# A gated expert layer: the first product comes out transposed, with the weight blocks stationary

## The chip, the cores and the metric

The kernel runs on one core of one Trainium2 chip. The metric is the device time of the whole program in microseconds (us), the median of a few runs. The program is written by hand for each engine: PE (matrix products), ACT (ScalarE), DVE (VectorE), POOL (GpSimd) and SP (which starts the plain DMAs). Each engine runs its own list of instructions in order; they meet only at semaphores.

## The reference

There are 2048 rows (4 batches of 512) of 512 numbers, `x`. Each row has a token number that chooses one of 4 experts. An expert is one 512 x 512 matrix `W` of `ctx_2048`, used three times:

```python
h = layernorm(x)
g = silu(h @ W.T);  u = h @ W.T          # the same product twice
y = (g * u) @ W.T
x = x + tanh(g_xattn) * y                # each row with its own expert
# second part, on every row
h2 = layernorm(x)
logits = h2 @ Wr + br + bonus            # 8 small experts, the top two, softmax weights
hid = relu(h2 @ Wd + bd)                 # 8 x 16 hidden numbers
x = x + tanh(g_ffn) * sum_e w[e] * (hid[e] @ Wu[e] + bu[e])
```

## The kernel before

**Tiling.** The kernel sorts the rows by expert and gathers them by indirect DMA in 16 tiles of 128 rows (`T`). A tile that holds rows of more than one expert is worked on once per expert, so there are `NP` = 19 pairs (tile, expert). Which expert a pair has is known only at run time: PE loads the number into a register (`expert_of`, L587) and addresses `w_hi` and `w_lo` with it.

**Precision.** Every fp32 operand of a large product is split in two fp16 halves, `hi` (ACT rounds) and `lo` (DVE subtracts), and a product is the sum of three matmuls: hi x hi, hi x lo and lo x hi. `w_hi` and `w_lo` hold the transposed weights, made once per expert at the start (`w_blocks` on PE, `high_parts` on ACT, `low_parts` on DVE and on POOL).

**One pair, engine by engine.** 
1. ACT normalises the tile into `h` (L803), PE transposes it into `ps_hT` (L656), ACT makes `hT_hi` (L789), DVE makes `hT_lo` (L1044, `hT_low`).
2. PE makes the first product in `ps_a` (`split_product`, L577 to L585): the transposed rows are stationary and 512 columns of the weights move, 12 matmuls; rows of the tile come out on the partitions.
3. ACT makes `silu` (L784), DVE the product `prod` (L1038).
4. PE transposes `prod` into `ps_pT` (`transpose_product`, L599), ACT makes `pT_hi` (L762), DVE makes `pT_lo` (L1072, `pT_low`).
5. PE makes the second product in `ps_y` with the same `split_product`; DVE adds it to the rows (L1056, `add_y`), whose tile and source numbers DVE's sequencer loads into registers (`place`, L1047).

**The second part** follows a tile when its last pair is surely done, LATE = 3 pairs later: statistics (DVE L1064, L1067, POOL L435 to L437), `h2` (ACT L775), its transposes (PE L664), `h2T_hi` and `h2T_lo` (L794, L1078), `hidden_product` (L606), the choice of two experts (DVE, POOL, ACT tanh), transposes of the weighted hidden numbers (L676), `low_rank_out` (L617), `add_low_rank` (DVE L1085), and the scatter (POOL L508).

**Order.** The order is written out by hand: each engine has a function `step(i, i0)`, called for i = 0, 1, 2, ...; in step i there stand the first product of pair i, the second of pair i-1, and second-part work of the tiles i-5, i-6, i-7 and i-8. On PE a full step is: `hidden_product`, `transpose_product` of pair i-1, first product of pair i, `low_rank_out`, transposes of `h` for pair i+1, transposes of `h2`, second product of pair i-1, transposes of the weighted numbers. On ACT: `pT_hi` of pair i-1, `wtT_hi`, `h2`, tanh, `silu` of pair i, `hT_hi` of pair i+1, `h2T_hi`, `h` of pair i+2. On DVE: the top two, `wtT_lo`, `pT_low` of pair i-1, `statistics1`, the weights of the two experts, `product` of pair i, `hT_low` of pair i+1, `h2T_low`, `add_low_rank`, `add_y` of pair i-1, `statistics2`, `hidden`. The first steps are mixed with the preparation of the weights (`w_blocks`, `top_norm`, `high_parts`, `square_sums`), and the last ones (`ending`, `draining` on DVE) have their own order. All eight PSUM banks are in use; the preparation borrows them by the list `w_banks` (L329).

Of the kernel before, what the change touches and what calls it, by code (L numbers as in the profile page):

```python
# [6 lines left out]
def bass_flamingo_gated_kernel(  # L7
# [53 lines left out]
    with ctx:  # L61
        def sb(name, shape, dt=fp32):
            return ctx.enter_context(nc.sbuf_tensor(name, shape, dt))

        def pb(name, shape, dt=fp32):
            return ctx.enter_context(nc.psum_tensor(name, shape, dt))

        def sem(name):
            return ctx.enter_context(nc.semaphore(name))
# [121 lines left out]
        silu = sb("silu", [P, D])  # L191
        prod = sb("prod", [P, D])
        pT_hi = sb("pT_hi", [P, KC, P], fp16)
        pT_lo = sb("pT_lo", [P, KC, P], fp16)
# [22 lines left out]
        ps_a = pb("ps_a", [P, D])  # L217
        ps_pT = pb("ps_pT", [P, KC, P])
# [55 lines left out]
        pT_done = sem("pT_done")  # L274
# [54 lines left out]
        w_banks = [[ps_pT, ps_y, ps_wT, ps_o], [ps_h2T, ps_pT, ps_y, ps_wT],  # L329
# [190 lines left out]
        def _(pe):  # L520
# [47 lines left out]
            for c in range(C):  # L568
                last = mm(ps_a[:, 0:NP], hot_slot[:, c, :], hot_pair[:, c, :],
                          start=(c == 0), stop=(c == C - 1))  # L570
# [4 lines left out]
            w_blocks(1, range(1, 3))  # L575

# [14 lines left out]
            def second_product(k, e):  # L591

                pe.wait_ge(pT_lo_done, k + 1)
                wait_last(pe, x1_done, k)
                if k == 0:
                    pe.wait_ge(*low_done(2, w_banks[2].index(ps_y)))
                split_product(ps_y, pT_hi, pT_lo, e).then_inc(y_done, 1)

            def transpose_product(k):  # L599

                pe.wait_ge(prod_done, k + 1)
                for c in range(KC):
                    last = tr(ps_pT[:, c, :], prod[:, c * P:(c + 1) * P], ident[:, :])  # L603
                last.then_inc(pT_done, 1)
# [26 lines left out]
            def step(i, i0, experts=None, meanwhile=None):  # L631
# [4 lines left out]
                if has_y and not has_a:  # L636
                    transpose_product(i - 1)
                if some(T, -3 - LATE, i0) and (has_y or some(NP, -2, i0)):
                    hidden_product(i - 3 - LATE)
                if has_y and has_a:  # L640
                    transpose_product(i - 1)
                if some(NP, 0, i0):
                    k = i
                    if i < E:
                        wait_low(pe, i)
                    pe.wait_ge(hT_lo_done, k + 1)
                    split_product(ps_a, hT_hi, hT_lo, e_now).then_inc(a_done, 1)
# [63 lines left out]
        def _(act):  # L711
# [43 lines left out]
            def step(i, i0, meanwhile=None):  # L755


                if some(NP, -1, i0):
                    k = i - 1
                    act.wait_ge(pT_done, k + 1)  # L760
                    wait_last(act, y_done, k)
                    a(pT_hi[:, :, :], ps_pT[:, :, :], ACT.Copy).then_inc(pT_hi_done, 1)  # L762
# [18 lines left out]
                if some(NP, 0, i0):  # L781
                    k = i
                    act.wait_ge(a_done, k + 1)
                    a(silu[:, :], ps_a[:, :], ACT.Silu, scale=inv_t[:, col(k)]).then_inc(silu_done, 1)  # L784
                if some(NP, 1, i0):
                    k = i + 1
                    act.wait_ge(hT_done, k + 1)
                    wait_last(act, a_done, k)
                    a(hT_hi[:, :, :], ps_hT[:, :, :], ACT.Copy).then_inc(hT_hi_done, 1)  # L789
                if some(T, -2 - LATE, i0):  # L790
                    k = i - 2 - LATE
                    act.wait_ge(h2T_done, k + 1)
                    wait_last(act, hid_mm, k)
                    a(h2T_hi[:, :, :], ps_h2T[:, :, :], ACT.Copy).then_inc(h2T_hi_done, 1)  # L794
# [45 lines left out]
        def _(dve):  # L840
# [114 lines left out]
            def pair_masks():  # L955

                dve.wait_ge(s_expert_f, 1)
                dve.wait_ge(s_rows_mm, 3)
                v.tensor_copy(in_pair[:, :], ps_a[:, 0:NP])
                v.tensor_copy(expert_i[:, :], expert_f[:, :]).then_inc(s_expert, 1)  # L960
# [133 lines left out]
            def step(i, i0, meanwhile=None):  # L1094
# [25 lines left out]
                if some(NP, -1, i0) and not ending:  # L1120
                    pT_low(i - 1)
# [62 lines left out]
            hT_low(1)  # L1184
            statistics1(3)
# [45 lines left out]
```

## Time and profile before

| what | value |
|---|---|
| median of 3 runs | 202.12 us (200.66 to 205.54) |
| the profiled execution | 201.35 us |
| its span, first to last instruction | 199.6 us |
| mean granted clock of PE | 0.947 |
| PE busy | 173.2 us (87%) |
| PE weight loads busy | 104.2 us (52%) |
| DVE busy | 154.8 us (78%) |
| ACT busy | 112.5 us (56%) |
| POOL busy | 100.5 us (50%) |
| DMA | 13.51 MB, mean 68 GB/s |

The span is shorter than the execution's time by what lies before the first and after the last instruction. A share of busy time is an average over the span: the first 35 us or so prepare routing and weights, the last 20 drain the second part. A matmul's duration contains the time until its result is written, so matmuls that follow one another overlap; their starts tell the pace. A name with a q behind the engine (PEldq, DVEq) is an operation of that engine's sequencer, which computes addresses, loads registers and waits; it isn't counted as busy.

### The profile page before, as it was taken

The page shows a single profiled execution, that of the slowest core. Times are in us where ns is not written, and L with a number is a line of the kernel's source. Part 1 is how long each engine was busy: PE and PEld are TensorE (multiplying, and loading weights), DVE is VectorE, ACT ScalarE, POOL GpSimd, SP SyncE. Part 2 cuts the span into 40 slices and gives each one's busy share as a digit, 9 for nine tenths or more (in the row PEclk, how much of TensorE's full clock was granted, in tenths as well). Part 3 has the DMA queues.
Part 4 walks back from the last instruction along what each step waited for, and adds up shares of the span by engine and source line. Part 5 has one row for each costly group of instructions (what it writes and reads, how often), then busy time and mean ns, then how long its engine had stood idle before and what let it go on. Part 6 is the DMA issues. An engine that isn't in the chain of part 4 may idle for free.

```text
span 199.6 us, 4088 instructions
## 1 busy us (share of the span) xinstructions
PE 173.2 (87%) x1074; PEld 104.2 (52%) x1074; DVE 154.8 (78%) x442; ACT 112.5 (56%) x223; POOL 100.5 (50%) x246
## 2 busy tenths in 40 slices
PE   1655897999996989999999999999999999977560
PEld 1644473655553546656566565665656656534210
DVE  4868597697768798898988989787877878668640
ACT  2595599984395274573755737557375572445200
POOL 4477856417344474475744736416245162445641
PEclk9995599999999999999999999999999999999955
DMA  4937672100310101203001010010010100101121
GB/s 134 395 123 225 231 221 73 53 3 11 95 48 9 53 0 53 57 0 107 21 35 53 3 53 25 34 53 23 34 53 2 56 28 25 53 3 53 54 105 53
DMA packets 6789, 13.51 MB, mean 68 GB/s; under 512 B 2392, under 2 KB 2520, under 8 KB 6768
## 3 DMA queue, kind: packets, MB, share of 16 engines
q0 software_dynamic: 2560, 8.39, 12.8%
q1 hardware_dynamic: 4208, 4.86, 7.3%
q8 instruction: 10, 0.16, 0.3%
q14 instruction: 11, 0.09, 0.1%
HBM read 9.06 MB, written 4.19 MB: 66 GB/s over the span
## 4 chain that ended last, share of the span: by engine, by line
PE 68%; POOL 7%; DMA 7%; DVE 6%; issue 6%; ACT 2%; SPq 2%; POOLq 1%; DVEq 0%
PE ps_y L582 8%; PE ps_y L584 8%; PE ps_y L583 8%; PE ps_a L582 7%; PE ps_a L584 6%; PE ps_a L583 6%; DMA xs<-in_x_dram,rows_of 4%; PE ps_pT L603 4%; PE ps_h2T L664 3%; PE ps_hT L656 3%; DMA bu_nat<-in_L_ffn_bu_dram 2%; POOL hot_slot L411 2%; PE ps_o L621 2%; POOL xs L418 2%; PE ps_o L624 2%
## 5 line engine op out<-in xcount | busy, mean ns | idle before, releaser
L435 POOL TENSOR_SCALAR ve<-mv 128x1 f32<-128x1 f32 x32 | 7.6, 238 | 59.6 <-DVE mv L1067 50.1
L775 ACT ACTIVATE h<-xs,mrs,rs 128x512 f32<-128x512 f32 x16 | 21.0, 1312 | 19.4 <-POOL mrs L437 19.4
L762 ACT ACTIVATE pT_hi<-ps_pT 128x512 f16<-128x512 f32 x19 | 11.3, 594 | 36.1 <-PE ps_pT L603 36.1
L582 PE MATMUL ps_y<-w_hi,pT_hi 128*128 x76 | 28.8, 379 | 2.0 <-DVE w_lo L931 1.2
L582 PE MATMUL ps_a<-w_hi,hT_hi 128*128 x76 | 29.3, 386 | 0.7 <-DVE hT_lo L1044 0.6
L583 PE MATMUL ps_a<-w_lo,hT_hi 128*128 x76 | 29.3, 386 | 0.0
L584 PE MATMUL ps_a<-w_hi,hT_lo 128*128 x76 | 29.2, 384 | 0.0
L583 PE MATMUL ps_y<-w_lo,pT_hi 128*128 x76 | 28.8, 379 | 0.0
L584 PE MATMUL ps_y<-w_hi,pT_lo 128*128 x76 | 28.8, 379 | 0.0
L1056 DVE SCALAR_TENSOR_TENSOR xs<-ps_y,y_t,xs 128x512 f32 x19 | 14.3, 750 | 12.1 <-PE ps_y L584 11.4
L436 POOL TENSOR_TENSOR rs<-ve,neg_half 128x1 f32<-128x1 f32 x32 | 19.7, 615 | 2.7
L508 POOL DMA_INDIRECT out_dram<-xs,rows_of x16 | 17.3, 1082 | 5.9 <-DVE xs L1085 3.5
L418 POOL DMA_INDIRECT xs<-in_x_dram,rows_of x16 | 17.0, 1064 | 3.7 <-issue 2.9
L803 ACT ACTIVATE h<-xs,mrs,rs 128x512 f32 (+1 forms) x19 | 15.5, 818 | 5.4 <-POOL mrs L437 4.2
L1038 DVE SCALAR_TENSOR_TENSOR prod<-ps_a,prod_bits,silu 128x512 f32<-128x512 f32 x19 | 14.0, 737 | 1.6 <-ACT silu L784 1.6
L784 ACT ACTIVATE silu<-ps_a,inv_bits 128x512 f32<-128x512 f32 x19 | 12.9, 677 | 4.2 <-PE ps_a L584 4.2
L1072 DVE TENSOR_TENSOR pT_lo<-ps_pT,pT_hi 128x512 f16<-128x512 f32 x19 | 13.1, 689 | 0.7 <-ACT pT_hi L762 0.3
L1085 DVE SCALAR_TENSOR_TENSOR xs<-ps_o,out_coef,xs 128x512 f32<-128x512 f32 x16 | 11.9, 741 | 2.2 <-PE ps_o L624 2.2
L664 PE MATMUL ps_h2T<-ident,h 128*128 128x128 f32 x64 | 9.9, 277 | 4.0 <-ACT h L775 4.0
L1044 DVE TENSOR_TENSOR hT_lo<-ps_hT,hT_hi 128x512 f16<-128x512 f32 x19 | 12.9, 679 | 0.3 <-ACT hT_hi L789 0.3
L719 ACT ACTIVATE sq_act<-w_nat 128x512 f32<-128x512 f32 x16 | 10.1, 632 | 5.0 <-DMA w_nat<-in_ctx_dram 4.5
L611 PE MATMUL ps_hid<-w_in_hi,h2T_hi 128*128 128x136 f16 x64 | 12.1, 223 | 0.4 <-DVE h2T_lo L1078 0.4
(205 smaller groups left out, 418.9 us busy)
## 6 DMA issues: line engine op xcount, KB each, us to landing
w_nat<-in_ctx_dram SPq DMA_DIRECT2D x4, 1024.0 KB, 8.0
xs<-in_x_dram,rows_of POOLq DMA_INDIRECT x16, 3.6
wd_nat<-in_L_ffn_Wd_dram SPq DMA_DIRECT2D x1, 256.0 KB
wu_nat<-in_L_ffn_Wu_dram SPq DMA_DIRECT2D x1, 256.0 KB
out_dram<-xs,rows_of POOLq DMA_INDIRECT x16, 2.9
b_in<-in_L_ffn_bd_dram SPq DMA_DIRECT2D x1, 64.0 KB
bu_nat<-in_L_ffn_bu_dram SPq DMA_DIRECT2D x3, 16.0 KB
tok_i<-in_itok_BxS_dram SPq DMA_DIRECT2D x1, 8.0 KB, 1.7
```

The costliest lines, as they stand in the source:

```text
L418: g.indirect_dma_start(out=xs[:, t, :], out_offset=None, in_=x_rows[:, :], in_offset=bass.IndirectOffsetOnAxis(ap=rows_of[:, t:t + 1], axi ...
L436: then(g.tensor_tensor(rs[:, n, k:k + 1], ve[:, n, k:k + 1], neg_half[:, :], ALU.pow))
L508: g.indirect_dma_start(out=out_rows[:, :], out_offset=bass.IndirectOffsetOnAxis(ap=rows_of[:, k:k + 1], axis=0), in_=x1[:, k, :], in_offse ...
L582: mm(ps[:, :], lhs_hi[:, kc, :], hi, start=(kc == 0), stop=False)
L583: mm(ps[:, :], lhs_hi[:, kc, :], lo, start=False, stop=False)
L584: last = mm(ps[:, :], lhs_lo[:, kc, :], hi, start=False, stop=(kc == KC - 1))
L664: last = tr(ps_h2T[:, c, :], h2[:, c, :], ident[:, :])
L775: a(h2[:, :, :], x1[:, col(k), :].rearrange("p o (q c) -> p c (o q)", c=KC), ACT.Identity, bias=mrs[:, 1, col(k)], scale=rs[:, 1, col(k)]) ...
L803: a(h[:, :], flat(xs[:, col(tile), :]), ACT.Identity, bias=mrs[:, 0, col(tile)], scale=rs[:, 0, col(tile)]).then_inc(normed1, 1)
L1038: v.scalar_tensor_tensor(prod[:, :], ps_a[:, :], prod_t[:, col(k)], silu[:, :], ALU.mult, ALU.mult).then_inc(prod_done, 1)
L1056: v.scalar_tensor_tensor(flat(x1[:, col(tile), :]), ps_y[:, :], y_t[:, col(k)], flat(xs[:, col(source), :]), ALU.mult, ALU.add).then_inc(x ...
L1072: v.tensor_tensor(pT_lo[:, :, :], ps_pT[:, :, :], pT_hi[:, :, :], ALU.subtract).then_inc(pT_lo_done, 1)
```

## The change

The first product is made with a 128 x 128 block of the weights stationary and the 128 transposed rows moving. It comes out transposed: the product's own columns on the partitions, the rows of the tile along the free axis, which is the layout that the second product needs. So `silu` and `prod` are transposed too, `transpose_product` goes, and with it its bank `ps_pT` and the semaphore `pT_done`. `pT_hi` and `pT_lo` are read from `prod` in SBUF in place of `ps_pT` in PSUM. `ps_a`, `prod`, `pT_hi` and `pT_lo` have two buffers each, used in turn; waits on use two pairs back are added. `pT_hi` and `pT_low` of pair i now stand in step i: on ACT behind `hT_hi` of pair i+1 and ahead of `h2T_hi`, on DVE behind `hT_low` of pair i+1 and ahead of `h2T_low`. The preparation borrows `ps_a[1]` where it borrowed `ps_pT`.

```diff
-        ps_a = pb("ps_a", [P, D])
-        ps_pT = pb("ps_pT", [P, KC, P])
+        ps_a = [pb(f"ps_a{b}", [P, KC, P]) for b in range(2)]
...
+            def first_product(k, e):
+
+                ps = ps_a[k % 2]
+                for c in range(KC):
+                    for kc in range(KC):
+                        hi = w_hi[:, bass.ds(e, 1), kc, c * P:(c + 1) * P].rearrange("p e n -> p (e n)")
+                        lo = w_lo[:, bass.ds(e, 1), kc, c * P:(c + 1) * P].rearrange("p e n -> p (e n)")
+                        mm(ps[:, c, :], hi, hT_hi[:, kc, :], start=(kc == 0), stop=False)
+                        mm(ps[:, c, :], hi, hT_lo[:, kc, :], start=False, stop=False)
+                        last = mm(ps[:, c, :], lo, hT_hi[:, kc, :], start=False, stop=(kc == KC - 1))
+                last.then_inc(a_done, 1)
...
-                split_product(ps_y, pT_hi, pT_lo, e).then_inc(y_done, 1)
-
-            def transpose_product(k):
-
-                pe.wait_ge(prod_done, k + 1)
-                for c in range(KC):
-                    last = tr(ps_pT[:, c, :], prod[:, c * P:(c + 1) * P], ident[:, :])
-                last.then_inc(pT_done, 1)
+                split_product(ps_y, pT_hi[k % 2], pT_lo[k % 2], e).then_inc(y_done, 1)
...
-                if has_y and not has_a:
-                    transpose_product(i - 1)
...
-                if has_y and has_a:
-                    transpose_product(i - 1)
...
-                    split_product(ps_a, hT_hi, hT_lo, e_now).then_inc(a_done, 1)
+                    if k > 1:
+                        pe.wait_ge(prod_done, k - 1)
+                    first_product(k, e_now)
...
-                if some(NP, -1, i0):
-                    k = i - 1
-                    act.wait_ge(pT_done, k + 1)
-                    wait_last(act, y_done, k)
-                    a(pT_hi[:, :, :], ps_pT[:, :, :], ACT.Copy).then_inc(pT_hi_done, 1)
...
+                    wait_last(act, prod_done, k)
+                    a(silu[:, :, :], ps_a[k % 2][:, :, :], ACT.Silu, scale=inv_t[:, col(k)]).then_inc(silu_done, 1)
...
+                if some(NP, 0, i0):
+                    k = i
+                    act.wait_ge(prod_done, k + 1)
+                    if k > 1:
+                        act.wait_ge(y_done, k - 1)
+                    a(pT_hi[k % 2][:, :, :], prod[k % 2][:, :, :], ACT.Copy).then_inc(pT_hi_done, 1)
...
             def product(k):
 
                 dve.wait_ge(silu_done, k + 1)
-                v.scalar_tensor_tensor(prod[:, :], ps_a[:, :], prod_t[:, col(k)], silu[:, :],
+                if k > 1:
+                    dve.wait_ge(pT_lo_done, k - 1)
+                v.scalar_tensor_tensor(prod[k % 2][:, :, :], ps_a[k % 2][:, :, :], prod_t[:, col(k)],
+                                       silu[:, :, :],
                                        ALU.mult, ALU.mult).then_inc(prod_done, 1)
...
-                v.tensor_tensor(pT_lo[:, :, :], ps_pT[:, :, :], pT_hi[:, :, :],
+                v.tensor_tensor(pT_lo[k % 2][:, :, :], prod[k % 2][:, :, :], pT_hi[k % 2][:, :, :],
                                 ALU.subtract).then_inc(pT_lo_done, 1)
...
                 if ending:
-                    pT_low(i - 1)
...
-                if some(NP, -1, i0) and not ending:
-                    pT_low(i - 1)
...
                 if some(NP, 1, i0):
                     hT_low(i + 1)
+                if some(NP, 0, i0):
+                    pT_low(i)
...
             product(0)
             hT_low(1)
+            pT_low(0)
             statistics1(3)
             router_bias()
```

## Rows read from the trace of the kernel before

**Rows 1.** The page, busy time of each engine, share of the span, number of instructions

```profile
PE 173.2 (87%) x1074; PEld 104.2 (52%) x1074; DVE 154.8 (78%) x442; ACT 112.5 (56%) x223; POOL 100.5 (50%) x246
```

**Rows 2.** Table by stretch: us, busy time of each engine (instructions), PEclk, DMA, GB/s

```profile
45.43:51.84 6.41, 6.36 (x35) 3.49 (x34) 4.25 (x10) 2.79 (x5) 4.99 (x11) 1.00 0.14 41
...
108.82:117.11 8.29, 8.29 (x57) 5.04 (x55) 7.44 (x21) 4.78 (x9) 4.55 (x12) 1.00 0.09 34
```

**Rows 3.** PE's timeline of one step: start us, duration us, engine, line, operation

```profile
113.59 0.38 PE L582 MATMUL ps_y<-w_hi,pT_hi 128*128 x1
...
115.97 0.38 PE L584 MATMUL ps_y<-w_hi,pT_lo 128*128 x1
...
116.40 0.22 PE L611 MATMUL ps_hid<-w_in_hi,h2T_hi 128*128 128x136 f16 x1
...
117.11 0.60 PE L603 MATMUL ps_pT<-ident,prod 128*128 128x128 f32 x4
...
117.55 0.38 PE L582 MATMUL ps_a<-w_hi,hT_hi 128*128 x1
```

**Rows 4.** DVE's timeline of the same step, from one add_y to the next

```profile
108.33 0.75 DVE L1056 SCALAR_TENSOR_TENSOR xs<-ps_y,y_t,xs 128x512 f32 x1 [0.44 <-PE ps_y L584]
...
111.31 0.69 DVE L1072 TENSOR_TENSOR pT_lo<-ps_pT,pT_hi 128x512 f16<-128x512 f32 x1
...
113.59 0.73 DVE L1038 SCALAR_TENSOR_TENSOR prod<-ps_a,prod_bits,silu 128x512 f32<-128x512 f32 x1
...
114.24 0.68 DVE L1044 TENSOR_TENSOR hT_lo<-ps_hT,hT_hi 128x512 f16<-128x512 f32 x1
...
114.84 0.68 DVE L1078 TENSOR_TENSOR h2T_lo<-ps_h2T,h2T_hi 128x512 f16<-128x512 f32 x1
...
115.44 0.74 DVE L1085 SCALAR_TENSOR_TENSOR xs<-ps_o,out_coef,xs 128x512 f32<-128x512 f32 x1
...
116.62 0.75 DVE L1056 SCALAR_TENSOR_TENSOR xs<-ps_y,y_t,xs 128x512 f32 x1 [0.44 <-PE ps_y L584]
```

**Rows 5.** ACT's timeline of the same step

```profile
109.46 0.60 ACT L762 ACTIVATE pT_hi<-ps_pT 128x512 f16<-128x512 f32 x1 [2.38 <-PE ps_pT L603]
...
111.43 1.32 ACT L775 ACTIVATE h<-xs,mrs,rs 128x512 f32<-128x512 f32 x1 [1.04 <-POOL mrs L437]
...
112.84 0.68 ACT L784 ACTIVATE silu<-ps_a,inv_bits 128x512 f32<-128x512 f32 x1
...
113.41 0.59 ACT L789 ACTIVATE hT_hi<-ps_hT 128x512 f16<-128x512 f32 x1
...
113.89 0.59 ACT L794 ACTIVATE h2T_hi<-ps_h2T 128x512 f16<-128x512 f32 x1
```

**Rows 6.** PE's sequencer at L582, L583 (ns min/median/max, first to last start); last: y(18)

```profile
L582 PEldq FUSED_REGOPS  x152: 46/46/51, 22.4 to 176.8; - x152
...
L583 PEldq ALU_OP  x152: 32/32/42, 22.5 to 177.0; - x152
...
L582 PEldq FUSED_REGOPS  x4: 46/46/46, 176.1 to 176.8; - x4
```

**Rows 7.** DVE's sequencer, 113 to 118 us: register loads of place, address of add_y

```profile
L1049 DVEq TENSOR_LOAD <-pair_tile_i x1: 301/301/301, 114.5 to 114.5; - x1
...
L1050 DVEq SEQ_ASSERT  x1: 23/23/23, 115.7 to 115.7; - x1
...
L1056 DVEq FUSED_REGOPS  x1: 99/99/99, 116.4 to 116.4; - x1
```

**Rows 8.** Timelines: h(3) on ACT; add_y of pairs 3, 16 and 18 on DVE

```profile
34.53 0.86 ACT L803 ACTIVATE h<-xs,mrs,rs 128x512 f32 x1
...
58.73 0.75 DVE L1056 SCALAR_TENSOR_TENSOR xs<-ps_y,y_t,xs 128x512 f32 x1 [1.55 <-PE ps_y L584]
...
166.35 0.75 DVE L1056 SCALAR_TENSOR_TENSOR xs<-ps_y,y_t,xs 128x512 f32 x1 [0.44 <-PE ps_y L584]
...
179.26 0.75 DVE L1056 SCALAR_TENSOR_TENSOR xs<-ps_y,y_t,xs 128x512 f32 x1 [1.09 <-PE ps_y L584]
```

More of the change, by code:

```diff
@@ L190, in bass_flamingo_gated_kernel @@
         hT_lo = sb("hT_lo", [P, KC, P], fp16)
[L191 to L194, printed above, removed]
+        silu = sb("silu", [P, KC, P])
+        prod = [sb(f"prod{b}", [P, KC, P]) for b in range(2)]
+        pT_hi = [sb(f"pT_hi{b}", [P, KC, P], fp16) for b in range(2)]
+        pT_lo = [sb(f"pT_lo{b}", [P, KC, P], fp16) for b in range(2)]
         h2 = sb("h2", [P, KC, P])
@@ L273, in bass_flamingo_gated_kernel @@
         prod_done = sem("prod_done")
-        pT_done = sem("pT_done")
         pT_hi_done = sem("pT_hi_done")
@@ L327, in bass_flamingo_gated_kernel @@
         AHEAD = 4
-        w_banks = [[ps_pT, ps_y, ps_wT, ps_o], [ps_h2T, ps_pT, ps_y, ps_wT],
+        w_banks = [[ps_a[1], ps_y, ps_wT, ps_o], [ps_h2T, ps_a[1], ps_y, ps_wT],
                    [ps_o, ps_y, ps_h2T, ps_wT], [ps_h2T, ps_wT, ps_o, ps_hid]]
@@ L568, in _ @@
             for c in range(C):
-                last = mm(ps_a[:, 0:NP], hot_slot[:, c, :], hot_pair[:, c, :],
+                last = mm(ps_a[0][:, 0, 0:NP], hot_slot[:, c, :], hot_pair[:, c, :],
                           start=(c == 0), stop=(c == C - 1))
@@ L783, in step @@
                     act.wait_ge(a_done, k + 1)
-                    a(silu[:, :], ps_a[:, :], ACT.Silu, scale=inv_t[:, col(k)]).then_inc(silu_done, 1)
+                    wait_last(act, prod_done, k)
+                    a(silu[:, :, :], ps_a[k % 2][:, :, :], ACT.Silu, scale=inv_t[:, col(k)]).then_inc(silu_done, 1)
                 if some(NP, 1, i0):
@@ L958, in pair_masks @@
                 dve.wait_ge(s_rows_mm, 3)
-                v.tensor_copy(in_pair[:, :], ps_a[:, 0:NP])
+                v.tensor_copy(in_pair[:, :], ps_a[0][:, 0, 0:NP])
                 v.tensor_copy(expert_i[:, :], expert_f[:, :]).then_inc(s_expert, 1)
```

## The prediction

> **Terms.** Pair k, step i and the products follow the code. *a* is the first product (hT times the expert's weights), *y* the second, *pT* the transposed product of silu and gate. T is the moment at which DVE starts add_y of one pair; the step is the distance to the next T.
>
> **What bounds the kernel now.** I first read the busy times: PE 173.2 of 199.6 us, no other engine above 78% [rows 1]. Then the table by stretch: from 108.82 to 117.11 PE is busy 8.29 of 8.29 us, DVE 7.44; the early steps, 6.41 us long, are full on PE too [rows 2]. PE's own timeline shows a step without a hole: y from 113.59, its last matmul at 115.97, two small transposes, the hidden product from 116.40, pT from 117.11, a from 117.55 [rows 3]. A 512-column matmul takes (115.97 - 113.59)/11 = 0.216 us, so 12 are 2.59. So PE sets the pace, and whoever shortens PE's work seems to win. But DVE is idle only 0.44 us before add_y (116.62) [rows 4], and everything behind T is a chain: T at 108.33, h2 on ACT at 111.43 (T+3.10), silu behind it at 112.84 (T+4.51), product at 113.59 (T+5.26) [rows 4, 5]. That slack, not PE's load, decides what a change may add.
>
> **Removed from PE.** Four transposes of pT: 117.55 - 117.11 = 0.44 us per pair [rows 3].
>
> **Added on PE: array time.** a has 48 matmuls of 128 columns in place of 12 of 512: the same columns, four times the weight loads. The hidden product shows what such a stream costs when its addresses are constants: 12 matmuls of 136 columns, each with new weights, in 117.11 - 116.40 = 0.71 us [rows 3], 59 ns each, 56 for 128 columns. So the array needs 48 x 0.056 = 2.67 us, +0.08. Net on the array: -0.36 us per step. If that were all, a step would be 7.93 us.
>
> **Added on PE: issue.** The expert is a register, so every block's address is computed by PE's sequencer: a fused register group (46 ns) and one ALU operation (32 ns), 152 of each now, one pair of them per three matmuls [rows 6]. For y(18), where the queue is empty, the four groups start from 176.1 to 176.8 [rows 6]: 0.7/3 = 0.23 us per three matmuls, of which 0.08 is arithmetic and the rest the issue of six instructions. Now this hides behind 3 x 0.216 = 0.65 us of array time. After the change there are 16 (block, kc) addresses in place of 4, still three matmuls each, and the array needs only 0.17 us for those. So a goes at issue pace: 15 x 0.23 + 0.2 = 3.7 us from its first address to its last matmul. Bounds: 2.67 (the sequencer is far enough ahead) and, as the reading 0.7 is rounded (0.6 to 0.8), 3.2 to 4.3. I take 3.7, since a's addresses can't be issued early: the hidden product stands before it and waits for h2T_lo, which ends only at 115.52 [rows 4], 0.9 before PE wants to start hidden.
>
> The Trainium skill, page "TensorE: Matmul & The Clock Gate", section "Back-to-back issue gap", says that in a real kernel, with a weight load per matmul, matmuls of 128 columns come about every 81 ns. The hidden product's 59 ns disagrees for constant addresses; by the page a would take an estimated 3.9 us, and the sum would come out nearly as mine, for another reason.
>
> **Moved: pT_hi and pT_lo.** pT_hi (ACT, 0.60) stood at the start of a step behind a 2.38 us idle; pT_lo (DVE, 0.69) started at 111.31, ahead of silu, where DVE had time [rows 4, 5]. Now both stand in the dense part behind product. In microseconds after T: product 5.26 to 5.99; pT_hi from 6.04 to 6.64 (hT_hi has left ACT by then); h2T_hi follows it 0.48 later, as it now follows hT_hi [rows 5], 6.52 to 7.11; hT_lo 5.91; pT_lo 6.68; h2T_lo 7.28; add_low_rank 7.88; DVE is free for add_y at 8.56. Sources change from PSUM to SBUF; no row shows the same operation both ways, so I leave the durations (a gain of up to 0.2 is the bound from below, +0.1 above).
>
> DVE's sequencer is a little later still. place() loads two registers after h2T_lo and add_low_rank are issued. Now: h2T_hi ends at 114.48, the loads begin at 114.5 and end with an assert at 115.7; after y's end the address arithmetic (116.4) puts add_y at 116.62 [rows 5, 7, 4]. That is 1.25 us of loads and checks plus 0.05 and 0.23. It is hidden today, y ends later. Afterwards h2T_hi ends at T+7.11, so add_y can start at 7.16 + 1.25 + 0.05 + 0.23 = T+8.68 at the earliest.
>
> **The three cycles of the steady step.** (1) DVE and ACT as just told: 8.68. (2) Through the issue: with X = end of h2T_lo, hidden is issued until X+0.6, a's last matmul starts at X+4.3, then low_rank_out 0.87, hT 0.44, h2T 0.44, y 2.37 and 0.65 to add_y: next T at X+9.2; and X is T+7.96. A T to the T after next costs 17.2, 8.6 per step. (3) T to h2's end 4.42, h2T, y and add_y 3.62: 8.04. The first wins: 8.68 against 8.29. Not counted: the new waits on prod_done, y_done and pT_lo_done, two pairs back, long satisfied (one short sequencer operation each), with the second buffers that make them so.
>
> **Early steps.** Up to T(3) at 58.73 [rows 8] the steps have no h2 chain and PE is full. a(2), a(3), a(4) each grow by 3.7 - 2.59 and lose 0.44: +0.7 a step, 2.1. On ACT, pT_hi(1) now waits for product(1) ahead of h at 34.53 [rows 8], and the norms and scales of expert 3 queue behind it; they gate a(2), which I put 0.5 late. T(3) comes 2.6 later. a(0) is at half clock and a(1) has a DMA's slack: nothing. Bounds: -1.1 (issue hidden, no ACT delay) to +4.
>
> **Steady.** T(3) to T(16) is 166.35 - 58.73 = 107.62 us [rows 8] in 13 steps; 13 x 8.68 = 112.8: +5.2.
>
> **End.** pT(18) no longer delays y(18), but y(18) then waits for add_y(17) to free ps_y: T(16) + 8.68 + 0.75 + 0.2, then 2.37 + 0.65 to add_y(18): T(16) + 12.6, against 179.26 - 166.35 = 12.91 [rows 8]. -0.3. Behind it the chain is as before.
>
> **Sum.** 2.6 + 5.2 - 0.3 = +7.5 us. The profiled execution took 201.35 us (span 199.6); the median of the runs shown, 202.12, is 0.8 above it. From there: 209.6; from the profiled one 208.9. I say 209.3.
>
> **Rivals.**
> A, *the issue runs ahead*: a costs 2.67, only the DVE and ACT cycle holds. Early steps +0.4, steady +5.2, end -0.3: 207.4. For it: now the sequencer is over a microsecond ahead of a. Against: h2T_lo comes later relative to y in the new order. 12%.
> B, *the issue is slower than shown*: registers now address the weight loads, where today they address the moving operand; no row shows such loads. At 0.30 us per group a is 4.8; then h2T_lo to hidden, a, low_rank_out, hT, hT_hi, hT_lo, pT_lo and back to h2T_lo is 9.5 a step: 13 x 9.5 - 107.6 = +16, early +6: 224. 8%.
> C, *not slower*: the slack swallows the moved pair. pT_lo leaves 0.61 us free ahead of the statistics and DVE idles 0.44 before T; if add_y is again released by y, cycle 3 sets 8.04 a step: early -1.1, 13 steps -3.1, end -0.3: 197.6. It decides if the path of cycle 1 is over 0.4 us shorter than the rows make it, and a's groups come under 0.17 us. Against: the freed 0.61 lies before silu, which is released by h2 and not by DVE. 8%; with half of each effect it ends within 2%: another 10%.
> D, my forecast, 62%: 206.5 to 212.5.
>
> **Numbers.** 2% is 4 us, about what a measurement tells from no change. Slower than 206.2: D, A and B, 82%. Same 11%, faster 7%. The range, 205 to 213.5, leaves out C and B and takes in the bounds of group pace and early steps.
>
> **What would show it.** Right: the address groups of a start 0.23 us apart and a spans 3.7 us; T to T is 8.6 to 8.7; PE idles before h2T or between a's matmuls, DVE not before add_y, or only for its register loads; T(3) near 61.3, T(16) near 174. [...]

## The result, and the profile after

The changed kernel takes **214.61 us** (median of 4 runs, 213.58 to 216.42) against 201.43 us (200.66 to 205.54) for the kernel before: the ratio is 1.067, 95% interval 1.059 to 1.076. It is slower, as forecast, but by 13.2 us between the medians where +7.5 was forecast. The two profiled executions took 213.58 and 201.35 us, +12.2; all the accounts below are made between these two.

First the busy times of the page: time, share of the span (now 211.8 us), number of instructions.

```profile
PE 183.8 (87%) x1682; PEld 128.7 (61%) x1682; DVE 157.7 (74%) x442; ACT 114.6 (54%) x223; POOL 100.2 (47%) x246
```

Against [rows 1] PE has 608 matmuls more and is busy 10.6 us more, though it has less to compute; DVE gains 3 us. No share says why the span grew. The moments at which add_y starts do. DVE's timeline, add_y of the pairs 0, 3, 16 and 18:

```profile
38.63 0.75 DVE L1062 SCALAR_TENSOR_TENSOR xs<-ps_y,y_t,xs 128x512 f32 x1 [1.12 <-issue]
63.47 0.75 DVE L1062 SCALAR_TENSOR_TENSOR xs<-ps_y,y_t,xs 128x512 f32 x1 [1.22 <-issue]
179.62 0.75 DVE L1062 SCALAR_TENSOR_TENSOR xs<-ps_y,y_t,xs 128x512 f32 x1
192.50 0.75 DVE L1062 SCALAR_TENSOR_TENSOR xs<-ps_y,y_t,xs 128x512 f32 x1 [1.07 <-PE ps_y L594]
```

Against [rows 8]: T(3) is 4.7 us later (63.47 for 58.73). T(3) to T(16) takes 116.15 us for 107.62, +8.5. T(16) to T(18) is 12.88 for 12.91. Behind T(18) come 19.3 us for 20.3; that stretch came out anywhere from 19.2 to 20.4 us in the kernels below, most of which share its code, so I don't count it to the change. **+4.7 early, +8.5 in the steady steps, -1.0 at the end** make the 12.2. And before add_y DVE now waits for "issue", its own sequencer, no longer for PE [rows 4].

One steady step, DVE's timeline from add_y to the next add_y:

```profile
126.05 0.75 DVE L1062 SCALAR_TENSOR_TENSOR xs<-ps_y,y_t,xs 128x512 f32 x1 [0.16 <-issue]
...
131.15 0.23 DVE L1146 TENSOR_SCALAR w_rep<-w,ffn_bits 128x24 f32<-128x24 f32 x1
131.41 0.75 DVE L1043 SCALAR_TENSOR_TENSOR prod<-ps_a,prod_bits,silu 128x512 f32<-128x512 f32 x1
132.08 0.68 DVE L1050 TENSOR_TENSOR hT_lo<-ps_hT,hT_hi 128x512 f16<-128x512 f32 x1
132.86 0.69 DVE L1078 TENSOR_TENSOR pT_lo<-prod,pT_hi 128x512 f16<-128x512 f32 x1
133.47 0.69 DVE L1084 TENSOR_TENSOR h2T_lo<-ps_h2T,h2T_hi 128x512 f16<-128x512 f32 x1
134.07 0.74 DVE L1091 SCALAR_TENSOR_TENSOR xs<-ps_o,out_coef,xs 128x512 f32<-128x512 f32 x1
134.97 0.75 DVE L1062 SCALAR_TENSOR_TENSOR xs<-ps_y,y_t,xs 128x512 f32 x1 [0.16 <-issue]
```

ACT's timeline of the same step:

```profile
129.15 1.31 ACT L771 ACTIVATE h<-xs,mrs,rs 128x512 f32<-128x512 f32 x1 [3.27 <-POOL mrs L435]
...
130.55 0.67 ACT L781 ACTIVATE silu<-ps_a,inv_bits 128x512 f32<-128x512 f32 x1
131.12 0.59 ACT L786 ACTIVATE hT_hi<-ps_hT 128x512 f16<-128x512 f32 x1
132.19 0.63 ACT L792 ACTIVATE pT_hi<-prod 128x512 f16<-128x512 f32 x1 [0.48 <-DVE prod L1043]
132.73 0.58 ACT L797 ACTIVATE h2T_hi<-ps_h2T 128x512 f16<-128x512 f32 x1
```

DVE's sequencer in that step (count, ns, first to last start), the register loads of place() and the address of add_y:

```profile
L1055 DVEq TENSOR_LOAD <-pair_tile_i x1: 324/324/324, 133.4 to 133.4; - x1
L1056 DVEq TENSOR_LOAD <-source_i x1: 354/354/354, 134.0 to 134.0; - x1
L1056 DVEq SEQ_ASSERT  x1: 23/23/23, 134.6 to 134.6; - x1
L1062 DVEq FUSED_REGOPS  x1: 99/99/99, 134.7 to 134.7; - x1
```

Read the three together: product, pT_hi, pT_lo, h2T_lo, add_low_rank stand back to back, the loads begin when h2T_hi has ended (133.31), and add_y follows their address arithmetic, at T+8.92. That is cycle 1 of the prediction, link by link. The first product on PE: its first and last matmul, then the next operation, and PE's sequencer computing its addresses (the last 12 of 16 groups):

```profile
126.01 0.22 PE L582 MATMUL ps_a<-hT_hi,w_hi 128*128 128x128 f16 x1
...
129.32 0.22 PE L584 MATMUL ps_a<-hT_hi,w_lo 128*128 128x128 f16 x1
129.60 0.38 PE L624 MATMUL ps_o<-wu_hi,wtT_hi 128*128 128x512 f16 x1
```

```profile
L582 PEldq FUSED_REGOPS  x12: 46/46/46, 126.4 to 129.1; - x12
```

12 groups whose starts lie 2.7 us apart are 0.24 to 0.25 us each, near the 0.23 forecast; this a takes 3.3 us from the start of its first to that of its last matmul, since the sequencer starts a little ahead. Over the run a takes 3.3 to 3.6 us in the steady steps and 3.8 to 3.9 in pairs 1 to 3. PE waits inside a, DVE waits for its register: which of the two costs time, a profile doesn't tell. The experiments do.

### The profile page after: what moved, and what is told of

It is laid out like the page before. It is cut to its first block, busy times and chain, and to the rows that moved or that the text cites. A ratio compares the mean times of both kernels' runs of the same rounds, so it can differ in the third digit from the quotient of the medians.

```text
span 211.8 us, 5809 instructions
## 1 busy us (share of the span) xinstructions
PE 183.8 (87%) x1682; PEld 128.7 (61%) x1682; DVE 157.7 (74%) x442; ACT 114.6 (54%) x223; POOL 100.2 (47%) x246
## 3 DMA queue, kind: packets, MB, share of 16 engines
HBM read 9.06 MB, written 4.19 MB: 63 GB/s over the span
## 4 chain that ended last, share of the span: by engine, by line
PE 49%; DVE 17%; issue 9%; POOL 7%; DMA 6%; ACT 4%; DVEq 2%; SPq 2%; POOLq 1%; ACTq 0%
PE ps_a L582 11%; PE ps_a L584 6%; PE ps_a L583 6%; PE ps_y L592 4%; PE ps_y L594 4%; PE ps_y L593 4%; DMA xs<-in_x_dram,rows_of 4%; DVE prod L1043 3%; ACT pT_hi L792 2%; DVE pT_lo L1078 2%; DVE xs L1062 2%; DMA bu_nat<-in_L_ffn_bu_dram 2%; PE ps_hT L657 2%; POOL hot_slot L409 2%; PE ps_hid L614 2%
## 5 line engine op out<-in xcount | busy, mean ns | idle before, releaser
L582 PE MATMUL ps_a<-hT_hi,w_hi 128*128 128x128 f16 x304 | 64.4, 227 | 1.7 <-DVE hT_lo L1050 1.5
L583 PE MATMUL ps_a<-hT_lo,w_hi 128*128 128x128 f16 x304 | 62.8, 222 | 0.0
L584 PE MATMUL ps_a<-hT_hi,w_lo 128*128 128x128 f16 x304 | 62.7, 222 | 0.0
L582 PEld LDWEIGHTS ps_a<-hT_hi,w_hi 128*128 x304 | 29.8, 98 | 14.5 <-issue 3.6
L583 PEld LDWEIGHTS ps_a<-hT_lo,w_hi 128*128 x304 | 30.4, 100 | 0.1
L584 PEld LDWEIGHTS ps_a<-hT_hi,w_lo 128*128 x304 | 29.6, 98 | 0.5
L434 POOL TENSOR_TENSOR rs<-ve,neg_half 128x1 f32<-128x1 f32 x32 | 18.8, 586 | 2.7
L792 ACT ACTIVATE pT_hi<-prod 128x512 f16<-128x512 f32 x19 | 12.0, 629 | 9.1 <-DVE prod L1043 9.1
L1139 DVE SCALAR_TENSOR_TENSOR w<-half_dif,half_tanh,half_sum 128x8 f32<-128x8 f32 x16 | 3.7, 228 | 16.0 <-ACT half_tanh L776 14.2
L1078 DVE TENSOR_TENSOR pT_lo<-prod,pT_hi 128x512 f16<-128x512 f32 x19 | 13.2, 692 | 2.5 <-ACT pT_hi L792 0.7
L614 PE MATMUL ps_hid<-w_in_hi,h2T_hi 128*128 128x136 f16 x64 | 12.2, 225 | 1.4 <-DVE h2T_lo L1084 1.2
```

The lines of the kernel that those rows point to most:

```text
L434: then(g.tensor_tensor(rs[:, n, k:k + 1], ve[:, n, k:k + 1], neg_half[:, :], ALU.pow))
L582: mm(ps[:, c, :], hi, hT_hi[:, kc, :], start=(kc == 0), stop=False)
L583: mm(ps[:, c, :], hi, hT_lo[:, kc, :], start=False, stop=False)
L584: last = mm(ps[:, c, :], lo, hT_hi[:, kc, :], start=False, stop=(kc == KC - 1))
L1078: v.tensor_tensor(pT_lo[k % 2][:, :, :], prod[k % 2][:, :, :], pT_hi[k % 2][:, :, :], ALU.subtract).then_inc(pT_lo_done, 1)
```

## Experiments

T and the step are as in the prediction; the steady step is (T(16) - T(4))/12. It was 8.29 us before and is 8.96 after (8.84 to 8.93 in ten steps, 9.49 and 9.20 in two). For the early part I use T(3) and, free of differences in the start, T(3) - T(0): 21.67 before, 24.84 after. A ratio is against executions of the kernel before from the same round of measurements, whose medians were 201.08 to 203.02 us.

### Constant addresses: static_a

```
-  hi = w_hi[:, bass.ds(e, 1), kc, c * P:(c + 1) * P].rearrange(...)
+  hi = w_hi[:, 0, kc, c * P:(c + 1) * P]        # lo likewise
```

> The first product always takes the weights of expert 0 (its result is not the reference's), so its 48 matmuls have constant addresses and PE's sequencer computes nothing for them; all else is as in the changed kernel. Chain theory (DVE and ACT behind add_y set the steady step): a spans about 2.7 us, the steady step stays at 8.9 us, T(3) to T(16) stays at 116; only the early steps, which PE sets, gain up to 0.7 each for a(2) to a(4): 211 to 213.5 us. Issue theory (PE's address issue sets the step): the step falls to 8.0 to 8.3, T(3) to T(16) to 104 to 108, the time to 200 to 204 us.

Measured: 211.27 us, ratio 1.044 (1.035 to 1.053). add_y of pairs 3 and 16:

```profile
60.13 0.75 DVE L1062 SCALAR_TENSOR_TENSOR xs<-ps_y,y_t,xs 128x512 f32 x1 [1.22 <-issue]
...
176.41 0.75 DVE L1062 SCALAR_TENSOR_TENSOR xs<-ps_y,y_t,xs 128x512 f32 x1
```

T(3) to T(16) is 116.28 us, against 116.15 in the changed kernel, with a now 2.6 us long. **The issue of a costs nothing in the steady step.** Early it costs all the more: T(3) - T(0) falls from 24.84 to 21.44, 3.4 us.

### The moved pair back in its old places: old_places, old_fix, static_old

```
 # ACT, step(i): pT_hi(i) behind hT_hi(i + 1)  ->  pT_hi(i - 1) at the start of the step
 # DVE, step(i): pT_low(i) behind hT_low(i + 1) ->  pT_low(i - 1) behind gwT
```

> The changed kernel with pT_hi and pT_lo issued one step later, where the kernel before had them (ACT at the start of a step, DVE behind gwT); the first product stays transposed with its 48 matmuls and PE's transposes of pT stay gone. Chain theory: the two leave the dense stretch behind product, so h2T_lo ends near T+6.6, add_low_rank near T+7.4, the register loads near T+7.9; the step is then set by the way through the issue of a, (2 x 8.24): 8.2 to 8.4, T(3) to T(16) 107 to 109, and the early delay through ACT's pT_hi(1) goes too: 203 to 207 us. Issue theory: a still takes 3.3 to 3.7 us and the step stays at 8.8 or more: 212 to 215 us.

> Both together: constant addresses of expert 0 in the first product (not the reference's result) and pT_hi and pT_lo in their old places. Chain theory: neither limit is left, a step is 7.95 to 8.1 us (PE's array 7.93, the cycle through h2's end 8.04): T(3) to T(16) 103.5 to 105.5, and about 197 to 200 us, below the kernel before. If some third thing holds the step (the second buffers, operands in SBUF, the waits), it stays above 8.3 and the time above 202.

old_places took 215.22 us (212.22 to 215.48), no better than the change, and static_old 208.87, ratio 1.023 (1.014 to 1.032): both times missed. (The traced execution of static_old took 209.97 us; only distances within its steady steps are read from it.) The steady step of old_places, 8.46 us, was near the 8.2 to 8.4 of the chain theory; that of static_old, 8.28, missed the 7.95 to 8.1, and something else held it (see the versions at the end). The loss in time was early: in old_places T(0) came at 41.66 and T(4) at 79.85. My edit had put ACT's pT_hi behind the high parts of experts 2 and 3, where the kernel before has it ahead of them. The table by stretch of old_places (us, busy times, PEclk, DMA, GB/s) shows what that brought:

```profile
33.70:36.90 3.20, 0.66 (x7) 0.42 (x5) 2.69 (x4) 3.16 (x7) 1.11 (x1) 1.00 0.25 78
36.90:41.60 4.70, 4.68 (x16) 2.13 (x17) 2.45 (x5) 3.33 (x12) 2.14 (x4) 0.64 0.08 10
```

PE had almost nothing to do for 3.2 us, waiting for pT(0), and then ran most of y(0) at the lower level, 1.2 GHz: its matmuls start 0.43 us apart instead of 0.216. The same befell y(1) and y(4): the clock was at half from 50.8 to 54.2 and from 74.7 to 78.1 us, and each took 3.6 to 3.8 us from first to last matmul instead of 2.4. From 47.4 to 51.2 us, ahead of y(1), PE had been busy for 1.08 of 3.80 us. old_fix puts pT_hi ahead of the high parts.

> As old_places, but ACT's pT_hi stands ahead of what step 1 and 2 do meanwhile (the high parts of experts 2 and 3), as in the kernel before; in old_places it stood behind them, and there PE idled 3.2 us before y(0) and ran y(0) at a granted clock of half. Reading of old_places: its steady step, T(4) to T(16) 101.6 us or 8.46 a step against 8.96 in the changed kernel and 8.29 before, was what the chain theory forecasts, and its early steps hid that. Chain theory: steady step again 8.4 to 8.5; with the early misplacement gone T(4) comes at 69 to 71 instead of 79.8: 203 to 206.5 us. If the early delay is not of that order on ACT but of the issue of a, T(4) stays above 74 and the time above 209.

Measured: 206.38 us, ratio 1.025 (1.019 to 1.030), T(4) at 70.92, step 8.46, all as expected: **undoing only the move of pT_hi and pT_lo gives back 8 us**, with 48 matmuls and register addresses still there. 0.5 us of the 0.67 us per step are this move.

But offsets within old_fix's step were not those of the kernel before: w8 started at T+5.00 (before 4.64) and product at T+5.76 (5.26). POOL, which prepares w8, had become slow at the time of pT_lo. arg8f on POOL over the 12 steady steps (ns min/median/max), old_fix and then, with the next experiment, old_inplace:

```profile
L468 POOL CAST arg8f<-arg x12: 190/709/716, 74.8 to 167.1; 128x8 f32<-128x8 uint32 x12
```

```profile
L468 POOL CAST arg8f<-arg x12: 180/189/191, 74.6 to 164.8; 128x8 f32<-128x8 uint32 x12
```

### Product in place, in PSUM: old_inplace and after_inplace

```
-  v.scalar_tensor_tensor(prod[k % 2][:, :, :], ps_a[k % 2][:, :, :], ...)
+  v.scalar_tensor_tensor(ps_a[k % 2][:, :, :], ps_a[k % 2][:, :, :], ...)
   # pT_hi and pT_lo read ps_a[k % 2]; a(k) waits for pT_lo(k - 2)
```

> As old_fix, but product writes over its own PSUM buffer instead of to SBUF, and pT_hi and pT_lo read it there: pT_lo again has one operand in PSUM, as in the kernel before (a(k) then waits for pT_lo(k-2)). Observed in old_fix: while DVE runs pT_lo from two SBUF operands at T+2.98, POOL's half_first takes 0.84 instead of 0.33 us, w8 starts at T+5.00 instead of 4.63 and product at 5.76 instead of 5.36. Theory (DVE with both operands in SBUF shuts POOL out): half_first back at 0.33, w8 at T+4.64, product at T+5.26 to 5.36; step 8.1 to 8.35 (T(4) to T(16) 97.5 to 100.2), time 201.5 to 205 us. Rival (PE's array and the issue of a hold the step, DVE only follows): the offsets go back, the step stays at 8.4 to 8.5, time 205 to 207 us.

> The changed kernel, its order kept, with product written over its own PSUM buffer and pT_hi and pT_lo reading it there instead of in SBUF. There pT_lo runs at T+6.8, when POOL has nothing that product waits for. Theory: only durations change, pT_hi 0.60 instead of 0.63 us; step 8.86 to 8.95, time 213 to 215 us. If the operands in SBUF were what makes the changed kernel slow: a step below 8.7 and a time below 212.

old_inplace: 203.98 us, ratio 1.013 (1.009 to 1.018); arg8f is back at 0.19 us, w8 at T+4.64, product at T+5.26, the step at 8.29, exactly that of the kernel before. So in the old places it was pT_lo's two operands in SBUF (prod and pT_hi, where the kernel before has ps_pT and pT_hi) that held POOL up for 0.52 us per step. The Trainium skill, page "SBUF — State Buffer", section "SBUF: two separate sides", says that a DVE operation with two SBUF inputs and a GpSimd operation that reads SBUF exclude each other from a shared pair of ports for a whole instruction. The trace agrees: 0.709 against 0.189 us for a cast from SBUF that starts 0.03 us after pT_lo.

after_inplace: 215.46 us, ratio 1.070 (1.065 to 1.076), step 8.95. In the changed kernel's order pT_lo runs at T+6.8, when nothing on POOL is urgent: there the operands in SBUF cost nothing in the steady step. pT_hi is 597 ns from PSUM and 629 from SBUF.

### The register load: place_early and static_place

```
+                if some(NP, -1, i0) and not ending:
+                    tile = tile_of(i - 1)          # between hT_low(i + 1) and pT_low(i)
...
-                        add_y(i - 1, *place(i - 1))
+                        add_y(i - 1, tile, source_of(i - 1))
```

> The changed kernel with one of DVE's two register loads for add_y (the tile) issued between hT_lo and pT_lo, where DVE's sequencer waits for pT_hi anyway; nothing else moves. Chain theory with the register loads as its last link (T+8.92): add_y is then released by the end of add_low_rank, T+8.66 to 8.72; T(4) to T(16) 103.9 to 105 instead of 107.5; in the early steps add_y(0) to add_y(2), which also wait for these loads, come 0.3 to 0.6 sooner: 210.5 to 212 us. If PE's y or the issue of a releases add_y, nothing changes: 213.5 to 215.5 us.

Measured: 210.07 us, ratio 1.044 (1.040 to 1.049). add_y of the pairs 0, 4 and 16:

```profile
37.64 0.75 DVE L1069 SCALAR_TENSOR_TENSOR xs<-ps_y,y_t,xs 128x512 f32 x1 [0.21 <-issue]
...
71.49 0.75 DVE L1069 SCALAR_TENSOR_TENSOR xs<-ps_y,y_t,xs 128x512 f32 x1 [0.21 <-PE ps_y L594]
...
176.04 0.74 DVE L1069 SCALAR_TENSOR_TENSOR xs<-ps_y,y_t,xs 128x512 f32 x1
```

104.55 us for 12 steps, 8.71, with add_low_rank at the same T+8.01: the loads were the last link, worth 0.25 us a step, from an edit that moves no arithmetic. T(0) comes 1.0 us sooner, but T(3) hardly (63.39). That says little, for this trace isn't like for like in the early steps. Its stretch from 41.82 to 45.24 (busy times of PE, PEld, DVE, ACT, POOL, then PEclk, DMA, GB/s):

```profile
41.82:45.24 3.42, 3.42 (x33) 3.33 (x32) 2.87 (x7) 2.00 (x5) 0.00 (x0) 0.50 0.00 0
```

The granted clock was 0.50, the 1.2 GHz level, where the changed kernel's trace has 1.00, and a(2) took 4.45 us instead of 3.88. From 36.5 to 40.2 us PE had been busy for 2.30 us here and 2.16 there, so no row shows why it fell. after_inplace and wait_moved show such a stretch too, single_ps, static_a and the next kernel don't.

> static_a and place_early together: the first product takes expert 0's weights at constant addresses (not the reference's result), and DVE loads the tile's register between hT_lo and pT_lo; the order of the changed kernel is kept. If the two account for the early loss, T(3) comes at 58.9 to 59.6 (60.13 with constant addresses alone, 63.39 with the early load alone, 58.73 before), the step is 8.67 to 8.72 as in place_early, and the time 206 to 208 us: what is left to the kernel before is then pT_hi and pT_lo in the dense stretch alone, 12 x 0.4 = 5 us. If a third cause sits in the early steps, T(3) stays above 60.

Measured: 206.36 us, ratio 1.025 (1.021 to 1.030), T(3) at 59.20, step 8.70. Both traces, static_a's and this one, have full clock up to T(3), and the early load brings T(3) from 60.13 to 59.20, 0.9 us sooner. Early, the issue of a and the register loads together leave 0.5 us of the 4.7. The remainder to the kernel before is the move of pT_hi and pT_lo: 12 x 0.40 = 4.8 us.

### The issue by itself: before48

```
 # kernel before; first product in 4 column blocks, transposes kept
+  mm(ps_a[:, cols], hT_hi[:, kc, :], hi, ...)    # hi = w_hi[:, bass.ds(e, 1), kc, cols]
```

> The kernel before, with one part of the change alone: the first product in 48 matmuls of 128 moving columns (16 register addresses instead of 4), not transposed, with the transposes of pT and every other instruction in its place. Chain theory, in which the issue counts only where PE cannot run ahead: in the steady step the sequencer has the time of the end of y and of pT's transposes to run ahead, so the step goes from 8.28 to 8.3 to 8.5; early steps cost 0.3 to 0.8 each: 202.5 to 206 us. Issue theory: a takes 3.7 instead of 2.6 us with nothing to hide it, 9.0 to 9.3 a step: 212 to 217 us.

Measured: 206.37 us, ratio 1.019 (1.012 to 1.025); T(3) at 61.16, step 8.52. In the steady step the sequencer runs ahead through y and the transposes, and a takes 2.6 to 2.9 us from first to last matmul (before 2.4); but PE was full, so 0.23 us more show in each step. Step and time are just above what I expected (8.5 and 206). Not all of the 0.23 is addresses: from static_a's 2.62 us I estimate 0.1 for the 48 matmuls themselves, and this layout with constant addresses wasn't run. So the split product costs 0.23 us a step where PE binds, and its 16 addresses nothing where DVE binds.

### Waits and buffers: wait_order, wait_moved, single_ps

> The changed kernel with the order of waits turned round at product (DVE), silu and pT_hi (ACT): the long satisfied wait for a buffer first, the wait that comes last carried by the instruction itself. Chain theory with the second wait as a link: product follows silu's end by 0.07 us instead of 0.19 and pT_hi loses about as little; step 8.75 to 8.85, T(4) to T(16) 105 to 106.2, the time 212.2 to 213.7 us. If an extra wait costs nothing: 107.5 and 214.6 as in the changed kernel.

> The changed kernel with product's second wait (for pT_lo two pairs back) taken up earlier in DVE's step, ahead of the statistics, so that product has only its wait for silu. In the steady step product starts 0.26 us after w_rep's start here and 0.15 after it in the kernel before, at the same T+5.10 and T+5.11. Theory: the second wait is this difference: product back at T+5.26, step 8.80 to 8.84 (T(4) to T(16) 105.6 to 106.2), time 212 to 213.8 us. Rival: the wait costs nothing once it is satisfied, and the 0.10 comes from product's own form (two buffers, output in the other layout): step 8.9 to 8.97, time as in the changed kernel.

> The changed kernel with one PSUM buffer for the first product instead of two (a(k) then waits for product(k-1)); prod and pT keep two. Chain theory: product(k-1) ends at T+6.0 and a(k) starts at T+8.9 in the steady step, so the second buffer buys nothing: T(4) to T(16) 107.5, within 0.5 us of the changed kernel, 214 to 215.2 us. If the buffer let a start early anywhere, T(3) or the steady step is later by a few tenths each and the time is 216 or more.

```
 # wait_order: product         - wait silu_done; wait pT_lo_done    + wait pT_lo_done; wait silu_done
 # wait_moved: product         - wait pT_lo_done   (stands ahead of statistics1 instead)
 # single_ps:  first_product   - ps = ps_a[k % 2]                   + ps = ps_a[0], a(k) waits for product(k - 1)
```

wait_order took 216.92 us, ratio 1.079 (1.074 to 1.085), step 9.06: slower, the opposite of what I expected. I had read the order the wrong way round. Of several waits the first is carried by the instruction and the others become sequencer operations ahead of it; the change had its late wait first, already the cheap way. Turned round, pT_hi starts at T+6.21 instead of 6.14, and everything behind it is later. wait_moved took 217.1 us, ratio 1.081 (1.076 to 1.087): the step is 9.09 us. product stayed at 0.19 us after silu's end, then in the last five steps fell to 0.50 us after it. So the second wait is not why product starts 0.10 us late in the changed kernel; in both kernels with pT_lo in its old place and product in place or before's form (old_inplace, before48) it starts at T+5.26 and 5.25, though old_inplace has the second wait too, and in after_inplace, in place but in the changed order, at 5.36. The delay goes with the order of the step. What makes these 0.10 us I can't say, nor why wait_moved loses more.

single_ps took 215.39 us, ratio 1.073 (1.066 to 1.080), T(3) 63.20, step 8.96, a little over the 214 to 215.2 us expected, but with the expected step: the second PSUM buffer buys nothing in this order.

### Versions built from the findings: old_best, best2, hybrid

> A version put together from the findings: old_inplace, and in addition PE keeps the expert's register of a pair for its second product (one register load per step less), DVE loads the tile's register between hT_lo and h2T_lo, product has a single wait. Theory: PE's array is full and its sequencer further ahead: a in 2.7 to 2.9 us, step 8.05 to 8.2 (T(4) to T(16) 96.6 to 98.4), T(4) at 69 to 71 as the early steps stay at issue pace: 200 to 203 us, level with the kernel before. If a's issue still binds in the steady step: 8.3 to 8.5 a step, 204 us or more.

> old_inplace, with PE keeping the expert's register for the second product, and without old_best's two edits on DVE. If the register kept is what helped old_best: T(4) 68.5 to 69.5 (old_inplace 70.65, old_best 68.85), step 8.1 to 8.28, 201.5 to 203.5 us. If old_best's gain came from DVE's earlier register load: as old_inplace, T(4) above 70 and 203.5 to 204.5 us.

> best2, in which pairs 0 to 3 take the first product as the kernel before did (12 matmuls of 512 columns, prod in SBUF, transposes into the second PSUM buffer) and pairs from 4 on as the change does (48 matmuls, no transposes, product in place). If the early loss is the issue of a: T(4) back at 66.7 to 67.3, as before; step 8.15 to 8.3, and after T(18) 19.2 to 19.4 instead of 20.3: 198.5 to 200.7 us, below the kernel before by 0.2 to 1.3%. If the early loss has another cause, T(4) stays near 69 and the time at 202 to 203.

```
 # old_best = best2, and on DVE the tile's register load ahead of h2T_low, product's second wait ahead of the statistics
 # best2 = old_inplace, and on PE
+                if k not in kept:                   # e of pair k kept for its second product
+                    kept.clear(); kept[k] = pe.value_load(...)
 # hybrid = best2, and
+                if k < 4: split_product(ps_a[0] ..., hT_hi, hT_lo, e)   # then transposes into ps_a[1]
```

old_best: 202.96 us, ratio 1.011 (1.006 to 1.016), T(4) 68.85, step 8.29. best2: 203.66 us, ratio 1.010 (1.006 to 1.015), T(4) 70.60, step 8.30. The kept register brought nothing: best2 is old_inplace (T(4) 70.65, step 8.29), so the 1.75 us by which old_best is earlier at T(4) came from its edits on DVE. In the medians 0.7 us of it show, less than the runs of either spread. Both miss the step hoped for, 8.05 to 8.2 and 8.1 to 8.28. **hybrid: 200.38 us, ratio 0.995 (0.993 to 0.997)**, 12 runs against 17: half a percent faster, the only version that isn't slower. add_y of pairs 4 and 16:

```profile
67.09 0.75 DVE L1085 SCALAR_TENSOR_TENSOR xs<-ps_y,y_t,xs 128x512 f32 x1 [1.02 <-PE ps_y L600]
...
166.38 0.75 DVE L1085 SCALAR_TENSOR_TENSOR xs<-ps_y,y_t,xs 128x512 f32 x1 [0.43 <-PE ps_y L600]
```

T(4) is at 67.09 (before 66.84): with the first four products in 12 matmuls the early loss is gone, T(3) - T(0) is 21.42. The steady step is 8.27, 0.02 below before. T(16) to T(18) takes 12.47 us for 12.91, which is all of the 0.4 us between the two traces. What I expected behind T(18), 19.2 to 19.4 us, was 20.35.

Why the freed 0.44 us of PE bring next to nothing even here is seen in old_inplace, in one steady step of PE (first and last matmul of a, transposes of `h2`, last matmul of y), ACT (`h2`) and DVE (two add_y):

```profile
112.37 0.75 DVE L1062 SCALAR_TENSOR_TENSOR xs<-ps_y,y_t,xs 128x512 f32 x1 [0.40 <-PE ps_y L594]
112.87 0.22 PE L582 MATMUL ps_a<-hT_hi,w_hi 128*128 128x128 f16 x1
...
115.47 1.33 ACT L777 ACTIVATE h<-xs,mrs,rs 128x512 f32<-128x512 f32 x1 [2.67 <-POOL mrs L435]
115.77 0.22 PE L584 MATMUL ps_a<-hT_hi,w_lo 128*128 128x128 f16 x1
...
117.20 0.60 PE L665 MATMUL ps_h2T<-ident,h 128*128 128x128 f32 x4
...
120.01 0.38 PE L594 MATMUL ps_y<-w_hi,pT_lo 128*128 x1
...
120.66 0.75 DVE L1062 SCALAR_TENSOR_TENSOR xs<-ps_y,y_t,xs 128x512 f32 x1 [0.39 <-PE ps_y L594]
```

`h2` is ready at 116.80, 0.4 us before PE gets to its transposes, and y releases add_y: PE sets the step again, and cycle 3 doesn't. a takes 2.90 us from first to last matmul where the kernel before needs 2.38. It starts 0.44 us sooner after T and ends 0.1 later, so the slower stream takes back what the transposes gave. best2 and hybrid look the same (a 2.7 to 3.3 us in the steady steps).

static_old has neither address arithmetic nor the moved pair, and still takes 8.23 to 8.35 a step. Its PE and its DVE in one of them:

```profile
122.12 0.60 PE L657 MATMUL ps_hT<-ident,h 128*128 128x128 f32 x4
122.72 0.66 PE L665 MATMUL ps_h2T<-ident,h 128*128 128x128 f32 x4
123.21 0.38 PE L592 MATMUL ps_y<-w_hi,pT_hi 128*128 x1
...
125.58 0.38 PE L594 MATMUL ps_y<-w_hi,pT_lo 128*128 x1
125.83 0.74 DVE L1091 SCALAR_TENSOR_TENSOR xs<-ps_o,out_coef,xs 128x512 f32<-128x512 f32 x1
126.49 0.74 DVE L1062 SCALAR_TENSOR_TENSOR xs<-ps_y,y_t,xs 128x512 f32 x1
```

Here h2T does wait for `h2` (T+4.48), the last matmul of y starts at 125.58, and 0.65 us later add_y could follow, at T+7.99: that is cycle 3, put at 8.04. But DVE has no idle time between product and add_y, and starts it 0.91 us after y's last matmul, behind add_low_rank. In this kernel w8 is late (T+4.99, pT_lo's operands in SBUF), and with it the whole chain on DVE: that sets the 8.25. Constant addresses with product in place, which would take both away, weren't run.

## Why the prediction was right in kind and wrong in size

- **Right:** the sign; array time of a (2.6 us with constant addresses, forecast 2.67); the pace of 0.23 to 0.24 us per address group; an issue that costs nothing in the steady step; cycle 1 as the one that binds, with the register loads as its last link. The granted clock was 1.00 from 63.47 to 179.62, so it has no part in the steady term. Rival A, issue ahead, fell with a(1) to a(3) at 3.8 to 3.9 us; rival B with the pace; rival C with the step.
- **a's length:** 3.3 to 3.6 us in the steady steps, not 3.7, as PE's sequencer was a few groups ahead. It changed nothing in the step. In the early steps, where it does count, a(1) to a(3) took 3.8 to 3.9 and a(4) 3.3.
- **The steady term, +5.2, was mis-sized: +8.5.** The failed step is the length of cycle 1, put at 8.68 us. Ten of the thirteen steps took 8.84 to 8.93 and one 8.65; together they make 2.0 of the missing 3.3 us. Link by link in the step shown (8.92): product starts at T+5.36 instead of 5.26 (a cause not found); pT_hi runs from 6.14 to 6.77, 0.63 us long instead of 0.60 (I had bounded the change by -0.2 and +0.1); h2T_hi ends at 7.26 instead of 7.11; the two loads and checks take 1.32 instead of 1.25 us (loads of 0.32 and 0.35 us where [rows 7] shows 0.30; in the steps of 8.84 to 8.87 both are 0.30 to 0.32).
- **The other 1.3 us are two long steps, 9.49 and 9.20.** In the first, product starts only at T+6.01. It does so in the kernel before as well, whose step is 8.33 there, as it still had the slack that the change uses up. What makes the other long I haven't followed. An error of 0.1 us in a link that repeats 13 times is 1.3 us: the range took in bounds for group pace and early steps, but not for the links of the cycle that I said would decide.
- **The early term, +2.6, was mis-sized: +4.7.** I had a(2) to a(4) at +1.1 each for issue, 3.3 in all, and that was right: 3.4 us up to T(3) (24.84 against 21.44). What failed is what I took off and left out. The transposes were to give back 1.3 us and gave 0.2 (21.67 to 21.44), because PE now waits where it didn't. Its two longest waits between T(0) and T(3), in PE's timeline after:

```profile
39.49 0.27 PE L537 MATMUL ps_hid<-ident,part_sq 128*1 128x128 f32 x1 [1.17 <-DVE part_sq L856]
...
48.71 0.23 PE L582 MATMUL ps_a<-hT_hi,w_hi 128*128 128x128 f16 x1 [0.59 <-DVE hT_lo L1050]
```

  PE idles 2.1 us between T(0) and T(3), where the kernel before idles 0.4. The first wait is for the norms of expert 3 (`part_sq`, on DVE right behind add_y(0)), which gate a(2): it starts 1.1 us later (40.46 for 39.37), where I had put 0.5. I also left out DVE's register loads ahead of add_y(0): pT_lo(0) moved in front of them, and T(0) came 1.6 us later, 1.0 of it for the loads (place_early). At T(3), with constant addresses, they are worth 0.9.
- **End:** -0.3 forecast from T(16) to T(18), 0.0 found. The -1.0 behind T(18) wasn't forecast and isn't explained; without it the trace would be 13.2 us longer, not 12.2.
- The Trainium skill's 81 ns per matmul of 128 columns (page "TensorE: Matmul & The Clock Gate", section "Back-to-back issue gap"), weighed in the prediction, doesn't hold for constant addresses: static_a starts 48 matmuls in 2.62 us, 56 ns each. In the issue-bound part the three matmuls of a 0.24 us group come to about 80 ns each, but from the issue with register addresses.

## What to carry to other kernels

Work that moves into a chain that closes with slack 0.4 us must be priced link by link, register loads and their order among the instructions included: here the freed engine was PE, and the bill was paid on ACT and DVE. Splitting a matmul into four multiplies its address arithmetic, too: here it cost nothing where DVE set the step, 0.2 us a step or more where PE did, and its full pace where the sequencer couldn't run ahead, as in the kernel's first steps. And when an operand moves from PSUM to SBUF, look at what POOL does at that moment. Before two traces are compared stretch by stretch, compare their granted clocks.

## What I had not expected of the hardware

- DVE's pT_lo with both inputs in SBUF lengthened a POOL operation beside it from 0.19 to 0.71 us; with one input in PSUM it did not.
- In old_places PE was busy for 0.66 of 3.20 us, and its granted clock then was half from 37.1 to 40.6 us: y(0)'s matmuls came 0.43 us apart there, 0.216 otherwise. In place_early it fell to half for 3.4 us behind a stretch no emptier than in the changed kernel, whose clock stayed full.
- A late wait written last, as a sequencer operation of its own, put pT_hi 0.07 us later; with the other waits turned round, 0.1 us a step in all (9.06 against 8.96).
- An ACT copy of 128x512 takes 597 ns from PSUM and 629 ns from SBUF.
